# Sum passes from tables of three bfloat16 parts in a graph network kernel on Trainium2

## The chip, the cores and the metric

One core of a Trainium2 chip runs the whole kernel. The metric is device time in microseconds, the median of several runs. The engines are PE (TensorE, matrix products), VectorE (DVE), ScalarE (ACT), GpSimd (POOL), and SyncE (SP), which mostly issues DMAs.

## The reference

6250 nodes with 256 features and 100000 edges go through four graph layers, each followed by a residual and a layer norm. The change touches the last, two graph convolutions:

```
def gcn_conv(x, src, dst, W, b, n):
    h = x @ W
    ...
    norm = dinv[s] * dinv[d]
    msg = h[s] * norm[:, None]
    out = jax.ops.segment_sum(msg, d, num_segments=n)
    return out + b
...
x = gcn_conv(x, src, dst, W1, b1, n)          # 256 -> 128
x = jax.nn.relu(batch_norm(x, g1, be1))
...
x = gcn_conv(x, src, dst, W2, b2, n)          # 128 -> 64
x = jax.nn.relu(batch_norm(x, g2, be2))
...
return jax.nn.relu(cat @ Wfc + bfc)
```

`dinv` is the inverse root of a node's degree; self loops are in. So for each node the rows `h * dinv` of its neighbours are summed, times its own `dinv`.

## The kernel before

Nodes lie in 50 windows (NW) of 128, a window's node on a partition. Edges are sorted by target into 832 chunks of up to 128 edges; a chunk's targets all lie in one window. Eight chunks are a batch, 104 batches (NBT) a pass. Attention passes named a1e, a2e, be and te come first; the trace's tile names begin with the stage's name.

The stages around the change, in order:

- **g1l**, `dense_chain` with GROUP = 5 windows a group: finishes the attention layer, normalises, multiplies by W1, and drains each window twice (`drain_v`, L2749 and L2750): scaled by `dinv` into `tile`, which SP stores window by window into the table in DRAM, and into `acc`, where the sums begin. The steps of all engines are interleaved over `t`; a group's work on an engine is put at a fixed distance (T2, APPLY, SMALL) behind its first window.
- **g1e**, `sum_pass` with width 128. POOL gathers, chunk by chunk, the 128 table rows of its edges (L1830) into a ring of 6 batches. ScalarE makes one-hot matrices of target places (L1856, L1859), ring of 4. PE multiplies one-hot by rows (L1846) into one of 4 PSUM tiles of a batch. VectorE adds each chunk's product to its window in `acc` (L1874), at a place read from a table of window numbers (`windows.load`, L1124, every 4 batches), each add behind the one before.
- **g2l**, `turned_norm` with a table: transposes the sums, batch-normalises, then goes through 13 banks of four windows: ScalarE applies scale, shift and ReLU (L2357), PE multiplies by W2 (L2346), VectorE scales into `tile` (L2390) and `acc` (L2391), SP stores the tile (L2318). `tile` is a ring of two banks.
- **g2e**, `sum_pass` with width 64; then `turned_norm` n2 without a table, and the final dense stage gfl.

Each stage ends with a barrier of all engines, so POOL's first gather comes after the last store of the table has landed.

The lines that keep VectorE's ring of tiles in g2l:

```
for q in range(BANKS):
    dve.wait_ge(s_product, q + 1)
    wait(dve, s_stored[q % 2], q // 2 * 16)
    ...
    dve.tensor_tensor(tile[...], ps, factors(q, width), ALU.mult)
    dve.tensor_tensor(sums(q, width), ps, factors(q, width), ALU.mult).then_inc(s_v, 1)
```

## Time and profile before

| | us |
|---|---|
| median of 3 runs | 9034.76 |
| lowest, highest | 9013.13, 9043.17 |
| the profiled execution's own time | 9060.25 |
| its span | 9058.5 |
| g1l, from its first products to g1e's first gather | 6640 to 6777 |
| g1e, from its first gather | 6777 to 7823 |
| g2l | 7826 to 7870 |
| g2e, from its first gather | 7870 to 8915 |
| n2 and the final stage | to the end |

The profile shows one execution. A line of a group of instructions has the source line, the engine, the operation, out<-in, shapes and count, then busy time and mean length, then how long the engine stood idle before them and what it waited for. In the timeline each row has start, duration, and in brackets the idle time before it. A float32 product is two records. The granted PE clock is given as a share of 2.4 GHz.

### The profile page before, as it was taken

To read this page: it belongs to the slowest core of one execution; us is meant where nothing else is said; L and a number is where in the kernel's file an instruction comes from. 1 tells how busy PE (TensorE), PEld (TensorE's weight loads), DVE (VectorE), ACT (ScalarE), POOL (GpSimd) and SP (SyncE) were. 2 spreads that over 40 slices of the span, in tenths; PEclk is the share of its full clock that TensorE was granted. 3 is DMA by queue.
4 is the path that set the end of the run, shared out by engine and by line. 5 is a ranking of instruction groups with operands and counts; after the bars stand their busy time and mean duration, and the time that the engine had idled before them with its cause. 6 is when DMAs were issued, how large, how long until landed. Compare 5 with 4: busy or idle time off the path is not lost. (4 is left out here: it accounts for less than half of the span.)

```text
span 9058.5 us, 137581 instructions
## 1 busy us (share of the span) xinstructions
PE 5911.9 (65%) x32642; PEld 4085.2 (45%) x32642; DVE 5896.6 (65%) x17613; ACT 4188.0 (46%) x12362; POOL 6066.1 (67%) x6034
## 2 busy tenths in 40 slices
PE   5776567777688778567776777777764444433336
PEld 3443344454555555444444454555453333333335
DVE  8998688888588888556666699899972222211113
ACT  6897433333466666233333344444433333333332
POOL 7897377775588888177775166666647777577773
PEclk9998877777577777777777899999985555555557
DMA  1343255553333433144543366656622222111111
GB/s 47 112 116 104 73 135 137 136 135 93 79 93 93 112 94 93 60 129 133 133 132 106 117 174 174 173 170 176 174 83 53 53 53 53 42 27 27 27 27 40
DMA packets 518707, 903.05 MB, mean 100 GB/s; under 512 B 149412, under 2 KB 258878, under 8 KB 517565
## 3 DMA queue, kind: packets, MB, share of 16 engines
q0 software_dynamic: 226304, 550.69, 23.5%
q1 hardware_dynamic: 291644, 343.69, 12.6%
q8 instruction: 301, 4.93, 0.2%
q14 instruction: 458, 3.74, 0.1%
HBM read 820.41 MB, written 73.07 MB: 99 GB/s over the span
## 5 line engine op out<-in xcount | busy, mean ns | idle before, releaser
L1292 POOL DMA_INDIRECT all_Y<-table,all_row x3328 | 3413.4, 1026 | 1469.4 <-issue 966.4
L1830 POOL DMA_INDIRECT all_Y<-table,all_row x1664 | 1570.1, 944 | 548.8 <-issue 506.5
L1846 PE MATMUL g1e_ps_u<-all_Y,g1e_onehot 128*128 128x128 f32 x1664 | 428.8, 439 | 619.3 <-DMA all_Y<-table,all_row 422.8
L1846 PE MATMUL g2e_ps_u<-all_Y,g2e_onehot 128*128 128x64 f32 x1664 | 406.6, 426 | 639.2 <-DMA all_Y<-table,all_row 569.3
L1343 PE MATMUL be_ps_u<-all_Y,be_onehot 128*128 128x258 f32 x1664 | 655.3, 547 | 252.2 <-DVE all_acc L1556 245.6
L1874 DVE TENSOR_TENSOR all_acc<-all_acc,g1e_ps_u 128x128 f32 x832 | 238.8, 287 | 809.9 <-PE g1e_ps_u L1846 703.5
L1874 DVE TENSOR_TENSOR all_acc<-all_acc,g2e_ps_u 128x64 f32 x832 | 183.6, 221 | 864.3 <-PE g2e_ps_u L1846 757.8
L1343 PE MATMUL a1e_ps_u<-all_Y,a1e_onehot 128*128 128x264 f32 x1664 | 694.2, 546 | 4.8 <-DVE all_acc L1556 2.8
L1846 PEld LDWEIGHTS g1e_ps_u<-all_Y,g1e_onehot 128*128 128x128 f32 x1664 | 370.6, 328 | 677.3 <-issue 353.3
L1846 PEld LDWEIGHTS g2e_ps_u<-all_Y,g2e_onehot 128*128 128x128 f32 x1664 | 370.4, 328 | 675.4 <-issue 349.2
L1343 PEld LDWEIGHTS be_ps_u<-all_Y,be_onehot 128*128 128x128 f32 x1664 | 391.8, 264 | 480.7 <-issue 348.2
L1324 PE MATMUL te_ps_q<-all_X,te_turned 128*128 x1664 | 503.6, 431 | 154.4 <-DVE te_product L1594 132.5
L1343 PE MATMUL te_ps_u<-all_Y,te_onehot 128*128 128x264 f32 x1664 | 530.9, 434 | 80.7 <-DVE all_Y L1544 80.0
L638 POOL TENSOR_SCALAR all_acc<-all_Y,all_acc 128x128 f16<-128x128 f16 x392 | 488.7, 1258 | 47.4 <-DVE all_acc L625 33.9
L736 PE MATMUL a2e_rank_ps_p<-all_X 128*128 128x512 f16 (+1 forms) x1568 | 474.3, 456 | 0.0
L1324 PEld LDWEIGHTS te_ps_q<-all_X,te_turned 128*128 128x128 f32 x1664 | 322.8, 209 | 291.4 <-issue 251.2
L1544 DVE TENSOR_TENSOR all_Y<-all_Y 128x128 f32<-128x128 f32 (+1 forms) x728 | 377.7, 519 | 74.3 <-ACT all_Y L1468 54.6
L671 PE MATMUL rank_dst_ps_p<-all_acc 128*128 128x512 f16 (+1 forms) x1568 | 352.1, 347 | 104.5 <-POOL all_acc L638 104.1
L1343 PEld LDWEIGHTS a1e_ps_u<-all_Y,a1e_onehot 128*128 128x128 f32 x1664 | 375.6, 256 | 81.8 <-issue 11.8
L1343 PE MATMUL a2e_ps_u<-all_Y,a2e_onehot 128*128 128x66 f32 x1664 | 350.7, 348 | 90.8 <-DVE all_acc L1556 90.6
L1859 ACT ACTIVATE g1e_onehot<-g1e_distance 128x1024 f32<-128x1024 f16 x104 | 109.9, 1057 | 636.3 <-PE g1e_ps_u L1846 636.1
L1859 ACT ACTIVATE g2e_onehot<-g2e_distance 128x1024 f32<-128x1024 f16 x104 | 109.8, 1056 | 636.3 <-PE g2e_ps_u L1846 636.2
(555 smaller groups left out, 15694.2 us busy)
## 6 DMA issues: line engine op xcount, KB each, us to landing
all_Y<-table,all_row POOLq DMA_INDIRECT x4992, 2.5
a1e_place_row<-places_dst SPq DMA_DIRECT2D x104, 256.0 KB
a2e_place_row<-places_dst SPq DMA_DIRECT2D x104, 256.0 KB
be_place_row<-places_src SPq DMA_DIRECT2D x104, 256.0 KB
te_place_row<-places_src SPq DMA_DIRECT2D x104, 256.0 KB, 3.6
all_Y<-lows_dst SPq DMA_DIRECT2D x98, 256.0 KB
all_Y<-codes_dst SPq DMA_DIRECT2D x98, 256.0 KB
all_acc<-lows_src SPq DMA_DIRECT2D x98, 256.0 KB
```

The source lines that it names most:

```text
L638: pool.tensor_scalar(self.row1[b][:, k, :], self.kept.half16, self.row[b][:, k:k + 1], self.kept.other_t[:, t * 8 + k:t * 8 + k + 1], ALU. ...
L671: last = pe.matmul(ps[:, 0:a1 - a0], self.row1[b][:, k, :], self.column1[b][:, k, a0:a1], start=first, stop=final)
L736: last = pe.matmul(ps[:, 0:a1 - a0], self.row1[b][:, k, :], self.column1[b][:, k, a0:a1], start=first, stop=final)
L1292: pool.indirect_dma_start(out=rows[:, r, k, :], out_offset=None, in_=table, in_offset=bass.IndirectOffsetOnAxis(ap=order.row[:, t * 8 + k: ...
L1324: last = pe.matmul(ps_q[pair % 2][:, j * HC:(j + 1) * HC], turned[b][:, k * P:(k + 1) * P], queries[:, bass.ds(windows.at(windows_j, chunk ...
L1343: pe.matmul(ps_u[k % 4][:, 0:R], onehot[b][:, k, :], summand[:, b, k, :], start=True, stop=True).then_inc(s_summed, 1)
L1544: dve.tensor_tensor(out[:, :, :, 0:C], rows[:, r, ks, value_c0:value_c0 + HC].rearrange("p k (h n) -> p k h n", h=H), bc(by, [P, 2, H, C]) ...
L1830: pool.indirect_dma_start(out=rows[:, r, k, :], out_offset=None, in_=table, in_offset=bass.IndirectOffsetOnAxis(ap=order.row[:, t * 8 + k: ...
L1846: last = pe.matmul(ps_u[u][:, k * width:(k + 1) * width], onehot[b][:, k, :], rows[:, r, k, :], start=True, stop=True)
L1859: act.activation(onehot[t % MARKS][:, :, :], distance[:, :, :], ACT.Relu, scale=-1.0, bias=1.0).then_inc(s_onehot, 1)
L1874: dve.tensor_tensor(mine, mine, ps_u[(t - 1) % AHEAD][:, k * width:(k + 1) * width], ALU.add).then_inc(s_added, 1)
```

## The change

The tables of g1e and g2e hold each value as three bfloat16 parts, side by side: the first is the value rounded, the second the rest rounded, the third what is left. A gathered row has 3 x width bfloat16 (768 and 384 bytes; before 512 and 256). The one-hot matrices are bfloat16 too. PE makes one product per chunk with 384 or 192 columns, and VectorE adds its three parts one after the other to the window in `acc`. PSUM is cut into 8 banks, one chunk each for width 128 and two for width 64; PE releases chunks to VectorE by pairs and asks for free banks by pairs. The ring of rows has 4 batches for width 128, 6 for 64.

The dense stages make the parts. In g1l `acc` is the only drain; then, group by group, ScalarE copies `acc` into the first part, VectorE subtracts it into `rest`, ScalarE copies `rest` into the second, VectorE subtracts that into the third, and SP stores the group. In g2l the same is done bank by bank. Both write from a ring of two `split` buffers.

```diff
-    RING, AHEAD, MARKS, U = 6, 4, 4, 4
+    MARKS, U = 4, 4
+    RING = 4 if width == 128 else 6
+    BANKS = 8
+    PER = 512 // (3 * width)
+    ROUND = BANKS * PER
...
-        rows = spare[:, 0:RING * 8 * width].rearrange("p (r k n) -> p r k n", k=8, n=width)
-        onehot = [m.sb(f"onehot{b}", [P, 8, P]) for b in range(MARKS)]
+        rows = Region(spare).take(RING * 8, 3 * width, dt=BF16).rearrange("p (r k) n -> p r k n", k=8)
+        onehot = [m.sb(f"onehot{b}", [P, 8, P], BF16) for b in range(MARKS)]
...
+        def sums(q):
+            x = q % ROUND
+            return ps_u[x // PER][:, x % PER * 3 * width:(x % PER + 1) * 3 * width]
...
-                    wait(pe, s_added, (t - AHEAD + 1) * 8)
                     for k in range(8):
                         if k % 4 == 0:
                             pe.wait_ge(s_rows[r][k // 4], t // RING * 64 + 64)
-                        last = pe.matmul(ps_u[u][:, k * width:(k + 1) * width], onehot[b][:, k, :], rows[:, r, k, :], start=True, stop=True)
-                    last.then_inc(s_summed, 1)
+                        if k % 2 == 0:
+                            wait(pe, s_added, (t * 8 + k + 2 - ROUND) * 3)
+                        last = pe.matmul(sums(t * 8 + k), onehot[b][:, k, :], rows[:, r, k, :], start=True, stop=True)
+                        if k % 2 == 1:
+                            last.then_inc(s_summed, 1)
...
-                        wait(dve, s_added, t * 8 + (k - 8))
-                        dve.tensor_tensor(mine, mine, ps_u[(t - 1) % AHEAD][:, k * width:(k + 1) * width], ALU.add).then_inc(s_added, 1)
+                        if k % 2 == 0:
+                            dve.wait_ge(s_summed, (q + 2) // 2)
+                        for j in range(3):
+                            wait(dve, s_added, q * 3 + j)
+                            dve.tensor_tensor(mine, mine, sums(q)[:, j * width:(j + 1) * width], ALU.add).then_inc(s_added, 1)
```

In g1l (`dense_chain` with `split_of`), with `first_part` and `second_part` at steps T2 + 7 and T2 + 8 behind a group's start on ScalarE, `split_rest` and `split_last` at T2 + 8 and T2 + 9 on VectorE, the store at T2 + 10 on SP:

```diff
-                dve.tensor_scalar(tile[:, 0:128], ps[:, 0:128], dinv_of[:, w:w + 1], None, ALU.mult)
                 return dve.tensor_scalar(acc[:, w * 128:w * 128 + 128], ps[:, 0:128], dinv_of[:, w:w + 1], None, ALU.mult)
...
+                def first_part(g):
+                    act.wait_ge(s_v, (g + 1) * GROUP)
+                    wait(act, s_stored[g % 2], g // 2 * 16)
+                    act.activation(split[:, g % 2, :, 0:width2], split_of(g), ACT.Copy).then_inc(s_first, 1)
...
+                def second_part(g):
+                    act.wait_ge(s_rest, g + 1)
+                    act.activation(split[:, g % 2, :, width2:2 * width2], rest[:, :, :], ACT.Copy).then_inc(s_second, 1)
...
+                def split_rest(g):
+                    dve.wait_ge(s_first, g + 1)
+                    dve.tensor_tensor(rest[:, :, :], split_of(g), split[:, g % 2, :, 0:width2], ALU.subtract).then_inc(s_rest, 1)
...
+                def split_last(g):
+                    dve.wait_ge(s_second, g + 1)
+                    dve.tensor_tensor(split[:, g % 2, :, 2 * width2:3 * width2], rest[:, :, :], split[:, g % 2, :, width2:2 * width2], ALU.subtract).then_inc(s_split, 1)
```

In g2l (`turned_norm`), on SP, on ScalarE and on VectorE:

```diff
                     for q in range(BANKS):
-                        sp.wait_ge(s_v, q + 1)
+                        sp.wait_ge(s_split, q + 1)
...
+                    for q in range(BANKS + 1):
+                        if q < BANKS:
+                            act.wait_ge(s_v, q + 1)
+                            wait(act, s_stored[q % 2], q // 2 * 16)
+                            act.activation(split[:, q % 2, 0:windows(q), 0:width], sums(q, width), ACT.Copy).then_inc(s_first, 1)
+                        if q > 0:
+                            act.wait_ge(s_rest, q)
+                            act.activation(split[:, 1 - q % 2, 0:windows(q - 1), width:2 * width], rest[:, 0:windows(q - 1), :], ACT.Copy).then_inc(s_second, 1)
...
-                        wait(dve, s_stored[q % 2], q // 2 * 16)
...
-                        dve.tensor_tensor(tile[:, q % 2, 0:windows(q) * width].rearrange("p (w n) -> p w n", n=width), ps, factors(q, width), ALU.mult)
-                        dve.tensor_tensor(sums(q, width), ps, factors(q, width), ALU.mult).then_inc(s_v, 1)
+                    for q in range(BANKS + 2):
+                        if q < BANKS:
+                            dve.wait_ge(s_product, q + 1)
+                            ps = ps_o[q % 2][:, 0:windows(q) * width].rearrange("p (w n) -> p w n", n=width)
+                            dve.tensor_tensor(sums(q, width), ps, factors(q, width), ALU.mult).then_inc(s_v, 1)
+                        if q > 1:
+                            k = windows(q - 2)
+                            dve.wait_ge(s_second, q - 1)
+                            dve.tensor_tensor(split[:, q % 2, 0:k, 2 * width:3 * width], rest[:, 0:k, :], split[:, q % 2, 0:k, width:2 * width], ALU.subtract).then_inc(s_split, 1)
+                            dve.wait_ge(s_split, q - 1)
+                        if 0 < q <= BANKS:
+                            k = windows(q - 1)
+                            dve.wait_ge(s_first, q)
+                            dve.tensor_tensor(rest[:, 0:k, :], sums(q - 1, width), split[:, 1 - q % 2, 0:k, 0:width], ALU.subtract).then_inc(s_rest, 1)
```

How this moves instructions is shown at three places. The first is VectorE at the start of g1e, before (TENSOR_LOAD reads the window numbers, ISA is the register instruction that computes a window's place, ps_u0 is a PSUM tile):

```order
L1124 TENSOR_LOAD all_window
L1874 ISA
L1874 TENSOR_TENSOR all_acc<-all_acc,g1e_ps_u0 128x128
L1874 ISA
L1874 TENSOR_TENSOR all_acc<-all_acc,g1e_ps_u0 128x128
```

And the same place with the change:

```order
L1124 TENSOR_LOAD all_window
L1887 ISA
L1887 TENSOR_TENSOR all_acc<-all_acc,g1e_ps_u0 128x128 x3
L1887 ISA
L1887 TENSOR_TENSOR all_acc<-all_acc,g1e_ps_u1 128x128 x3
```

Where one add followed each register instruction, three do, and the next chunk is in the next bank.

The second is VectorE in g2l's banks, before (two banks):

```order
L2390 TENSOR_TENSOR g2l_tile<-g2l_ps_o0,all_small 128x256
L2391 TENSOR_TENSOR all_acc<-g2l_ps_o0,all_small 128x256
L2390 TENSOR_TENSOR g2l_tile<-g2l_ps_o1,all_small 128x256
L2391 TENSOR_TENSOR all_acc<-g2l_ps_o1,all_small 128x256
```

And with the change, the first four banks' drains (L2450), the subtractions into `rest` (L2459) and the third parts (L2454):

```order
L2450 TENSOR_TENSOR all_acc<-g2l_ps_o0,all_small 128x256
L2450 TENSOR_TENSOR all_acc<-g2l_ps_o1,all_small 128x256
L2459 TENSOR_TENSOR g2l_rest<-all_acc,g2l_split 128x256
L2450 TENSOR_TENSOR all_acc<-g2l_ps_o0,all_small 128x256
L2454 TENSOR_TENSOR g2l_split<-g2l_rest,g2l_split 128x4x64
L2459 TENSOR_TENSOR g2l_rest<-all_acc,g2l_split 128x256
L2450 TENSOR_TENSOR all_acc<-g2l_ps_o1,all_small 128x256
L2454 TENSOR_TENSOR g2l_split<-g2l_rest,g2l_split 128x4x64
L2459 TENSOR_TENSOR g2l_rest<-all_acc,g2l_split 128x256
```

The tile's drain is gone, and a bank's third part stands behind the drain of the bank two later.

The third is ScalarE in g2l. Before, its work there ends with the thirteen L2357 (in the changed kernel L2408). With the change first parts (L2414) and second parts (L2417) follow:

```order
L2408 ACTIVATE all_Y<-all_Y,g2l_column 128x512 x12
L2408 ACTIVATE all_Y<-all_Y,g2l_column 128x256
L2414 ACTIVATE g2l_split<-all_acc 128x4x64 x2
L2417 ACTIVATE g2l_split<-g2l_rest 128x4x64
L2414 ACTIVATE g2l_split<-all_acc 128x4x64
L2417 ACTIVATE g2l_split<-g2l_rest 128x4x64
L2414 ACTIVATE g2l_split<-all_acc 128x4x64
L2417 ACTIVATE g2l_split<-g2l_rest 128x4x64
```

The first parts of banks 0 and 1 come together; from then on the first part of a bank stands ahead of the second part of the bank before.

## Rows read from the trace of the kernel before

**Rows 1.** The page: each engine's busy time, share of the span and instructions.

```profile
PE 5911.9 (65%) x32642; PEld 4085.2 (45%) x32642; DVE 5896.6 (65%) x17613; ACT 4188.0 (46%) x12362; POOL 6066.1 (67%) x6034
```

**Rows 2.** Windows: part of a1e, of a2e, g1l, part of g1e, of g2e.

```profile
core 0: us, PE busy (x) PEld busy (x) DVE busy (x) ACT busy (x) POOL busy (x), PEclk, DMA share, GB/s
1200.00:1800.00 600.00, 469.96 (x2229) 299.04 (x2229) 526.21 (x1584) 236.38 (x767) 453.95 (x475) 0.77 0.51 136
2400.00:3000.00 600.00, 491.07 (x4051) 336.67 (x4050) 484.93 (x1987) 410.02 (x1328) 482.51 (x386) 0.71 0.39 98
6640.00:6777.00 137.00, 95.27 (x584) 81.65 (x584) 109.36 (x335) 52.20 (x214) 48.06 (x60) 0.90 0.18 66
6790.00:7790.00 1000.00, 412.88 (x1603) 356.72 (x1602) 230.19 (x802) 350.89 (x901) 755.89 (x802) 0.50 0.21 53
...
7890.00:8890.00 1000.00, 390.99 (x1600) 356.20 (x1600) 176.58 (x800) 344.05 (x883) 755.76 (x801) 0.50 0.15 27
```

**Rows 3.** Timeline rows of g1e and g2e, and groups by line and form.

```profile
7302.91 2.05 PE L1846 MATMUL g1e_ps_u<-all_Y,g1e_onehot 128*128 128x128 f32 x8 [3.09 <-DMA all_Y<-table,all_row]
7307.74 0.94 POOL L1830 DMA_INDIRECT all_Y<-table,all_row  x1 [0.30 <-issue]
7309.95 3.30 DVE L1874 TENSOR_TENSOR all_acc<-all_acc,g1e_ps_u 128x128 f32 x8 [6.34 <-PE g1e_ps_u L1846]
7883.62 2.76 DVE L1874 TENSOR_TENSOR all_acc<-all_acc,g2e_ps_u 128x64 f32 x8 [16.56 <-PE g2e_ps_u L1846]
L1859 ACT ACTIVATE g1e_onehot<-g1e_distance 128x1024 f32<-128x1024 f16 x104 | 109.9, 1057 | 636.3 <-PE g1e_ps_u L1846 636.1
L736 PE MATMUL a2e_rank_ps_p<-all_X 128*128 128x512 f16 x784 | 401.4, 519 | 0.0
```

**Rows 4.** Adds and loads by line (ns min/median/max), and a dependent VectorE chain in g2l.

```profile
L1874 DVEq FUSED_REGOPS  x1664: 57/57/57, 6790.7 to 8914.7; - x185
L1874 DVE TENSOR_TENSOR all_acc<-all_acc,g1e_ps_u x832: 286/286/289, 6790.8 to 7822.3; 128x128 f32 x167
L1124 DVEq TENSOR_LOAD <-all_window x188: 1096/2101/2350, 1152.3 to 8904.9; - x188
7841.35 0.19 DVE L2375 TENSOR_TENSOR g2l_parts<-g2l_parts 128x26 f32<-128x26 f32 x1
7841.57 0.19 DVE L2376 TENSOR_TENSOR g2l_parts<-g2l_parts,g2l_stats 128x26 f32<-128x26 f32 x1
```

**Rows 5.** Timeline of g2l: ScalarE's L2357, banks 10 and 12, the first gather.

```profile
7843.75 9.06 ACT L2357 ACTIVATE all_Y<-all_Y,g2l_column 128x512 f32<-128x512 f32 x13 [7.62 <-DVE g2l_column L2384]
7863.75 0.42 DVE L2390 TENSOR_TENSOR g2l_tile<-g2l_ps_o,all_small 128x256 f32<-128x256 f32 x1 [0.95 <-PE g2l_ps_o L2346]
7864.09 0.41 DVE L2391 TENSOR_TENSOR all_acc<-g2l_ps_o,all_small 128x256 f32<-128x256 f32 x1
7865.46 0.43 DVE L2390 TENSOR_TENSOR g2l_tile<-g2l_ps_o,all_small 128x256 f32<-128x256 f32 x1 [0.95 <-PE g2l_ps_o L2346]
7866.57 0.29 DVE L2390 TENSOR_TENSOR g2l_tile<-g2l_ps_o,all_small 128x128 f32<-128x128 f32 x1 [0.36 <-DMA table<-g2l_tile]
7866.78 0.28 DVE L2391 TENSOR_TENSOR all_acc<-g2l_ps_o,all_small 128x128 f32<-128x128 f32 x1
7870.26 0.99 POOL L1830 DMA_INDIRECT all_Y<-table,all_row  x1 [27.20 <-SPq L1823]
```

**Rows 6.** g1l's drains and tail on the timeline, and prices from groups by form.

```profile
6760.99 0.34 DVE L2750 TENSOR_SCALAR all_acc<-g1l_ps_o,all_small 128x128 f32<-128x128 f32 x1
6761.25 0.34 DVE L2749 TENSOR_SCALAR g1l_tile<-g1l_ps_o,all_small 128x128 f32<-128x128 f32 x1
6773.25 0.35 DVE L2749 TENSOR_SCALAR g1l_tile<-g1l_ps_o,all_small 128x128 f32<-128x128 f32 x1 [2.12 <-DMA table<-g1l_tile]
L2742 DVE TENSOR_TENSOR all_Y<-all_acc 128x1280 f32<-128x1280 f32 x10 | 14.9, 1492 | 0.3
L2357 ACT ACTIVATE all_Y<-all_Y,g2l_column 128x256 f32<-128x256 f32 x1 | 0.6, 586 | 0.0
```

More of the change, by code:

```diff
@@ L2006, in dense_chain @@
             cuts2 = [(a, min(a + 512, width2)) for a in range(0, width2, 512)]
-            tile = m.sb("tile", [P, 2, B.table_width])
+            if split_of is None:
+                tile = m.sb("tile", [P, 2, B.table_width])
+            else:
+                tile = None
+                split = m.sb("split", [P, 2, GROUP, 3 * width2], BF16)
+                rest = m.sb("rest", [P, GROUP, width2])
+                s_first, s_rest, s_second, s_split = (m.sem(x) for x in ("first", "rest", "second", "split"))
         if norm:
@@ L2044, in _ @@
                     w = t - T2 - 2
-                    if B is not None and is_window(w):
+                    g = group_at(t - T2 - 10)
+                    if split_of is not None and g is not None:
+                        sp.wait_ge(s_split, g + 1)
+                        sp.dma_start(B.table[g * GROUP * P:(g + 1) * GROUP * P, :].rearrange("(w p) n -> p w n", p=P), split[:, g % 2, :, :]).then_inc(s_stored[g % 2], 16)
+                    if split_of is None and B is not None and is_window(w):
                         sp.wait_ge(s_v, w + 1)
@@ L2249, in _ @@
                 for t in range(STEPS):
+                    if split_of is not None and group_at(t - T2 - 9) is not None:
+                        split_last(group_at(t - T2 - 9))
                     if B is not None and is_window(t - T2 - 2):
                         drain2(t - T2 - 2)
+                    if split_of is not None and group_at(t - T2 - 8) is not None:
+                        split_rest(group_at(t - T2 - 8))
                     if A is not None and is_window(t - T1 - 2):
@@ L2290, in turned_norm @@
             W = m.sb("W", [P, width])
-            tile = m.sb("tile", [P, 2, 4 * width])
+            split = m.sb("split", [P, 2, 4, 3 * width], BF16)
+            rest = m.sb("rest", [P, 4, width])
+            s_first, s_rest, s_second, s_split = (m.sem(x) for x in ("first", "rest", "second", "split"))
             ps_o = [m.ps(f"ps_o{b}", [P, 512]) for b in range(2)]
@@ L2755, in gnn_kernel @@
                         second=Step(sources=[(x3, 0, P), (x3, P, P)], weights=[W[:, 0, :], W[:, 1, :]], width=128, drain_v=drain_v,
-                                    table=tables[128], table_width=128))
-        sum_pass(nc, c, "g1e", order, tables[128], 128, acc, T2)
-        turned_norm(nc, c, "g2l", 128, acc, dinv_of, T1, (g_b1, g_g1, g_be1), g_w2, tables[64], 64)
-        sum_pass(nc, c, "g2e", order, tables[64], 64, acc, T2)
+                                    table=split_tables[128], table_width=384),
+                        split_of=lambda g: acc[:, g * GROUP * 128:(g + 1) * GROUP * 128].rearrange("p (w n) -> p w n", n=128))
+        sum_pass(nc, c, "g1e", order, split_tables[128], 128, acc, T2)
+        turned_norm(nc, c, "g2l", 128, acc, dinv_of, T1, (g_b1, g_g1, g_be1), g_w2, split_tables[64], 64)
+        sum_pass(nc, c, "g2e", order, split_tables[64], 64, acc, T2)
         turned_norm(nc, c, "n2", 64, acc, dinv_of, T2, (g_b2, g_g2, g_be2), ones_row=True)
```

34 lines of the change are left out of this document (19 added, 15 removed).

## The prediction

> **What bounds the kernel now.** I read the page's busy shares, then stretches of time (windows), then the groups and single instructions of the stages that change. No engine is busy more than 67% of the span [rows 1], so the shares name no bound; each stage must be read by itself. Both sum passes, g1e and g2e, show the same picture [rows 2]: POOL 756 of 1000 us busy, VectorE 230 and 177, PE 413 and 391, ScalarE 351 and 344. POOL is busy for 0.94 us, then 0.30 us in "issue", then starts the next gather [rows 3]; 1000 us hold 802 gathers, so they start 1.25 us apart, and nothing is waited for. 832 gathers make 1040 us a pass, and that is the pass. PE waits for landings, VectorE for PE [rows 3]. It makes no difference that g1e gathers 512 bytes a row and g2e 256: the pace is one.
>
> The stages between are another matter. In g1l VectorE is busy 109 of 137 us [rows 2]. In g2l's second half PE makes one bank of four windows in 1.71 us, VectorE drains it with two instructions [rows 5], and stores stay behind that.
>
> **The change part by part.**
>
> *Products.* Four chunks' float32 products, two records each, take 2.05 us [rows 3]. A product becomes one bfloat16 product with 384 or 192 columns. The nearest row, 128x512 in float16, has 0.519 us [rows 3]; even at that, eight products take 4.2 us of a batch's 9.98. PE waited anyhow: worth 0. PE's clock is already granted at 0.50 in both passes, its lower level of 1.2 GHz [rows 2], so less work there has little to lose.
>
> *Adds.* VectorE now adds three parts per chunk. Eight adds take 3.30 us in g1e, so one takes (3.30 - 0.29) / 7 = 0.43 us from start to start: 0.286 of work, 0.057 of a register instruction that computes the window's place, and two hand-overs of 0.04 [rows 3, 4]. The second and third add reuse that place, and only wait for the add before. A chain of such dependent instructions in g2l leaves 0.03 us between them [rows 4], so I take 0.286 + 0.035 = 0.32 us. A chunk costs 0.43 + 2 x 0.32 = 1.07 us, a batch 8.6, plus a quarter of the 2.1 us load of window numbers [rows 4]: 9.1 us against POOL's 9.98. In g2e eight adds take 2.76 us [rows 3], 0.54 less, so 24 take 1.6 less: 7.5. Covered, with 0.9 us a batch to spare; the rings of rows (now four batches) and banks only need to bridge a half batch. The tail of a pass moves by under 1 us: there are three times the adds, but the first pair starts before all four products are done. Worth 0 for both passes, 1 us either way.
>
> *Gathers.* Same number and same indices. Rows grow to 768 and 384 bytes. a1e's rows are 1056 bytes, and its gathers come every 600 / 475 = 1.26 us [rows 2]. Worth 0.
>
> *g1l.* VectorE loses one drain per window. The start-to-start distance of L2750 and the next L2749 is 0.26 us [rows 6], so 1.3 us a group. It gains two subtractions of 640 elements a group: half of 1280 elements at 1.492 is 0.75 [rows 6], and with a small instruction's 0.19 [rows 4] on top of the half's own fixed part it is at most 0.85. Net +0.2 to +0.4 us for nine groups: +2.5 us. ScalarE gets two copies of 640 elements a group, halfway between 256 at 0.586 and 1024 at 1.057 [rows 3, 6], 0.82; it is busy 52 of 137 us, and that idle time hides them. Without that cover they cost up to 15 us. The tenth group is at the tail, where nothing hides it. Today the last drain there waits 2.12 us for a store [rows 6], which goes, about 2.4 us gained in all. Then come copy, subtract, copy, subtract: 0.82 + 0.75 + 0.82 + 0.75 and four hand-overs, 3.3 us. Then the store: 480 KB where there was 64 KB. a1e moves 136 GB/s at half DMA share [rows 2]; 416 KB more are 3.1 us at that rate and 1.6 at twice that; I take 2.5. Tail +3.4, g1l in all **+6 us**, from -1 to +15.
>
> *g2l.* Here is the cost. The table is written from a ring of two buffers, as before. But ScalarE's queue is now: first part of bank q, then second part of bank q-1 (the order above). The first part of bank q waits for the store of bank q-2. The store of bank q-2 is only issued after VectorE's last subtraction of that bank. What is queued behind that wait on ScalarE is the second part of bank q-1, which VectorE's last subtraction of q-1 needs, and so the store of q-1. So this is a loop with one store's whole latency per bank: store, first copy, second copy, last subtraction. The store's latency stands in the trace: bank 10's L2391 ends at 7864.50, and bank 12, which waits for its buffer, starts at 7866.57 [rows 5]: 2.07 us, hand-overs included, for 128 KB. I add 0.15 for 192 KB. A copy of 256 elements lies between a quarter of 1024 at 1.057, 0.264 [rows 3], and 0.586, the row with scale and bias [rows 6]; I take 0.47, nearer the row of the same size. The subtraction has 0.41, as L2391 [rows 5], and 0.07 go for hand-overs. Period: 2.22 + 0.94 + 0.48 = **3.64 us** against 1.71.
>
> ScalarE can't begin before its thirteen L2357 are done, 7843.75 + 9.06 = 7852.81 [rows 5]. Bank 0's first copy, subtraction, second copy and last subtraction (0.47, 0.41, 0.47, 0.41 and hand-overs) hand it over at 7854.75. Eleven periods later, at 7894.8, bank 11; the last, half a bank, 1.1 us later, 7895.9. Today that point is 7866.78 + 0.28 = 7867.06, and the first gather starts 3.2 us after it [rows 5]. So g2l costs **+29 us**. Lower end: copies 0.264 each, no more for the larger store, VectorE at its 0.34 start to start, a period of 3.0 and +22. Upper end: copies 0.586, the store 2.6, a period of 4.3 and +36.
>
> That a store costs about two microseconds whatever its size is also in the Trainium skill ("DMA: Bandwidth & Descriptors", Anatomy of one DMA): a fixed 2.0 us, mostly the wait for the written bytes' receipt, and bytes by 436 GB/s. By that, 192 KB would be an estimated 2.45 us, the period 3.87 and g2l +31; the trace's 2.07 us for 128 KB lies a little under its 2.3.
>
> **The sum.** Profiled execution: 9060.25 + 6 (g1l) + 29 (g2l) + 0 (passes) = 9095 us. It is 25.5 above the median of the runs, 9034.76, so I predict **9070 us** there, +35, with the ends of g1l and g2l 9056 to 9086. About 0.3%, 27 us, is what a measurement here can tell from no change; the border is 9062, so the forecast is slower, but close to it.
>
> **The rivals.**
>
> *A: the store loop does not bind g2l, and the time is the same.* If the buffer were free when ScalarE asks, PE would go on at 1.71 us a bank; g2l would only lose the late start of ScalarE and the last bank's four steps, some 5 us. With g1l that gives 9035 + 11 = **9046 us**. For it: today the same ring of two makes VectorE wait only once [rows 5]. Against it: today a bank's store is issued right after its drain, a bank and a half before the buffer is wanted; now it is issued by the step behind the one that waits. It decides at a period of 3.0 us: under that g2l costs less than 21 us, and the whole less than 27.
>
> *B: VectorE becomes the bound of g1e.* If the second and third add cost what the first does (0.43), a batch takes 24 x 0.43 + 0.53 = 10.85 us against 9.98: 0.87 x 104 = 90 us more, **9160 us**. g2e stays covered (1.6 less, 9.25). It begins above (9.98 - 0.53 - 8 x 0.43) / 16 = 0.376 us an add, a gap of 0.09 where I take 0.035. For it: no row shows two dependent adds from PSUM without the register instruction. Against it: the short chain, and 0.43 itself is 0.286 + 0.057 + two gaps of 0.04.
>
> *C: a busy VectorE slows the gathers.* VectorE goes from 23% to some 85%. In a2e POOL needs 600 / 386 = 1.55 us a gather, with VectorE 81% busy; in a1e 1.26 with VectorE 88% busy [rows 2]. So it is not the share but the kind of instruction. At a2e's pace both passes would take 1664 x 0.304 = 506 us more, **9576 us**. The adds here have a1e's kind: float32, one operand in PSUM. The Trainium skill ("SBUF — State Buffer", SBUF: two separate sides) has a rule for this: VectorE and GpSimd hold a shared pair of ports in turn, and VectorE takes it in its two-port modes or with two SBUF inputs. By that rule these adds, with one SBUF input, leave POOL alone; a1e agrees.
>
> *D: faster.* g1l would have to gain more than g2l loses: all drains' 13 us without the subtractions would not do it. Only the spread of the runs can make it look so.
>
> **How the numbers follow.** Forecast 0.76, A 0.12, B 0.08, C 0.02, D 0.02. Inside the forecast, by its ends and the runs' spread of 30 us, about a quarter falls below 9062. Slower: 0.76 x 0.76 + 0.10 = 0.68; same: 0.18 + 0.12 = 0.30; faster 0.02. The range 9040 to 9105 holds the forecast with some spread of runs, and A; B and C, and the outer tails, are left out.
>
> **What would show it.** Right: gathers in both passes 1.25 us apart, with POOL 756 of 1000 us; VectorE 80 to 90% busy in g1e, its second and third adds 0.32 us apart; in g2l one store each 3.6 us, ScalarE waiting for the DMA before each first part, and PE idle; g1l's first gather some 6 us later after its start, g2l's some 29 later. Wrong: g2l's banks at 1.7 us (A); g1e's gathers in groups with waits for PE (B); gathers over 1 us long while the adds run (C).

## The result and the profile after

| | us |
|---|---|
| before, median of 7 runs | 9039.02 (9013.13 to 9053.15) |
| after, median of 7 runs | 9073.52 (9044.98 to 9076.28) |
| ratio, with its 95% interval | 1.0033 (1.0021 to 1.0045) |
| after, the profiled execution | 9044.98, span 9043.3 |

The change costs 34.5 us, 0.33%. The profiled execution of the changed kernel happens to be the fastest of its seven, and that of the kernel before, 9060.25, lies above all seven shown here. Compared as totals, the two profiles would say "15 us faster". That difference lies ahead of the change: g1l begins 46.9 us earlier in the profile of the changed kernel, and 32 of these are in a2e, which the change doesn't touch (1283.4 us from its first product of gathered rows to its last in the one, 1251.0 in the other). So the stages must be compared one by one, each from its own landmark:

| stage, from what to what | before | after | difference | predicted |
|---|---|---|---|---|
| g1l, first add to `all_X` to first gather | 124.16 | 129.63 | +5.5 | +6 |
| g1e, first gather to g2l's first SyncE transfer | 1048.27 | 1048.19 | -0.1 | 0 |
| g2l, that transfer to the next first gather | 44.85 | 71.01 | +26.2 | +29 |
| g2e, first gather to n2's first SyncE transfer | 1048.28 | 1048.24 | 0.0 | 0 |
| sum | | | +31.6 | +35 |

The 3 us between this sum and the medians' 34.5 can't be assigned: the interval of the ratio stands for 19 to 41 us.

The page's engine row of the changed kernel, the counterpart of [rows 1]:

```profile
PE 5532.6 (61%) x30978; PEld 3533.3 (39%) x30978; DVE 6740.9 (75%) x20924; ACT 4210.4 (47%) x12408; POOL 6037.3 (67%) x6034
```

PE lost 379 us of work and VectorE gained 844. Neither lengthens the passes: POOL, which didn't change, still paces both. Windows of g1e and g2e of the changed kernel (start and end, us, then PE, PEld, VectorE, ScalarE, POOL busy, PE clock, DMA share, GB/s), and g1e's groups by line:

```profile
6740.00:7740.00 1000.00, 289.94 (x800) 86.70 (x800) 686.72 (x2392) 359.18 (x923) 756.31 (x801) 0.50 0.30 79
7860.00:8860.00 1000.00, 162.00 (x801) 86.76 (x802) 529.81 (x2400) 358.45 (x921) 755.88 (x802) 0.50 0.19 40
```

```profile
L1838 POOL DMA_INDIRECT all_Y<-split,all_row x829 | 783.7, 945 | 252.5 <-issue 252.5
L1887 DVE TENSOR_TENSOR all_acc<-all_acc,g1e_ps_u 128x128 f32 x2487 | 714.2, 287 | 334.6 <-PE g1e_ps_u L1855 159.4 <-DVE all_acc L1887 54.7 <-issue 4.1
L1855 PE MATMUL g1e_ps_u<-all_Y,g1e_onehot 128*128 128x384 bf16 x832 | 301.5, 517 | 749.6 <-DMA all_Y<-split,all_row 381.8 <-issue 367.8
```

Against [rows 2]: PE 413 to 290, VectorE 230 to 687, POOL 756 both times, with 801 or 802 gathers in 1000 us. POOL's only idle time is "issue", so no gather waited for a free buffer. VectorE still waits for PE 159 us, where it waited 703 before. Not all of that is slack: VectorE's own load of window numbers (2.1 us every fourth batch) and the hand-over after PE lie inside these waits.

The passes' near-zeros in the table hide a shift at the pass's end. The end of g1e, first in the kernel before, then in the changed one:

```profile
7814.50 0.94 POOL L1830 DMA_INDIRECT all_Y<-table,all_row  x1 [0.30 <-issue]
7820.57 2.00 DVE L1874 TENSOR_TENSOR all_acc<-all_acc,g1e_ps_u 128x128 f32 x5 [0.20 <-DVE all_acc L1874]
7825.41 0.33 SPq L2313 DMA_DIRECT2D g2l_vector<-in_L_gnn_b  x1
```

```profile
7781.16 2.00 DVE L1887 TENSOR_TENSOR all_acc<-all_acc,g1e_ps_u 128x128 f32 x6 [0.21 <-DVE all_acc L1887]
7783.93 0.34 SPq L2364 DMA_DIRECT2D g2l_vector<-in_L_gnn_b  x1
```

Counted from the first gather, the last add ends 2.0 us later than before (1047.4 us instead of 1045.4), but g2l's first transfer follows 0.8 us behind it instead of 2.8. In the kernel before that transfer comes 10.91 us after the last gather's start, and so it does, within 0.01 us, in g2e of both kernels and of every undisturbed variant below. What sets this time stays open. In g1e of the changed kernel it is 9.4 us, and the adds end the pass.

g2l is where the time went. Two periods of its banks in the changed kernel, VectorE, ScalarE and the store queue:

```profile
7812.57 0.43 DVE L2454 TENSOR_TENSOR g2l_split<-g2l_rest,g2l_split 128x256 bf16<-128x256 f32 x1
7813.02 3.82 SPq L2369 DMA_DIRECT2D split<-g2l_split  x2
7813.03 0.42 DVE L2459 TENSOR_TENSOR g2l_rest<-all_acc,g2l_split 128x256 f32<-128x256 f32 x1
7813.37 0.42 DVE L2450 TENSOR_TENSOR all_acc<-g2l_ps_o,all_small 128x256 f32<-128x256 f32 x1
7815.26 0.42 ACT L2414 ACTIVATE g2l_split<-all_acc 128x256 bf16<-128x256 f32 x1 [2.72 <-DMA split<-g2l_split]
7815.58 0.40 ACT L2417 ACTIVATE g2l_split<-g2l_rest 128x256 bf16<-128x256 f32 x1
7816.01 0.42 DVE L2454 TENSOR_TENSOR g2l_split<-g2l_rest,g2l_split 128x256 bf16<-128x256 f32 x1 [2.22 <-ACT g2l_split L2417]
```

Here is the loop (L2414 makes a first part, L2417 a second, L2454 a third): third part of bank 0 at 7812.57, its store right behind it, ScalarE waiting 2.72 us for that store, first part of bank 2, second part of bank 1, third part of bank 1 at 7816.01, 3.44 us after that of bank 0. From bank 0 (7812.57) to bank 11 (7850.17) the third parts come 3.42 us apart on average. The waits of the tile `g2l_split` (us, times):

```profile
  DMA split<-g2l_split: 29.8, 11
  ACT g2l_split L2417: 25.0, 12
```

Eleven waits of 2.7 us each for a store, and twelve of VectorE for ScalarE behind them. In [rows 5] there was one wait for a store, of 0.36 us.

g1l's tail in the changed kernel, with the chain of four steps that nothing hides:

```profile
6727.84 0.74 ACT L2205 ACTIVATE g1l_split<-all_acc 128x640 bf16<-128x640 f32 x1 [1.71 <-DVE all_acc L2818]
6728.60 0.82 DVE L2286 TENSOR_TENSOR g1l_rest<-all_acc,g1l_split 128x640 f32<-128x640 f32 x1 [0.80 <-ACT g1l_split L2205]
6729.46 0.74 ACT L2209 ACTIVATE g1l_split<-g1l_rest 128x640 bf16<-128x640 f32 x1 [0.89 <-DVE g1l_rest L2286]
6730.23 0.83 DVE L2290 TENSOR_TENSOR g1l_split<-g1l_rest,g1l_split 128x640 bf16<-128x640 f32 x1 [0.80 <-ACT g1l_split L2209]
6731.08 0.36 SPq L2067 DMA_DIRECT2D split<-g1l_split  x1
6735.74 1.05 POOL L1838 DMA_INDIRECT all_Y<-split,all_row  x1 [19.73 <-SPq L1831]
```

Copy, subtraction, copy, subtraction: 3.2 us, then a store of 480 KB that takes 2.9 us to land (64 KB took 1.5 before), then the first gather.

### The profile page after: what moved, and what is told of

It reads as the page before. It is cut to its first block and busy times, and to the rows that moved or that the text cites. A ratio compares the mean times of both kernels' runs of the same rounds, so it can differ in the third digit from the quotient of the medians.

```text
span 9043.3 us, 138372 instructions
## 1 busy us (share of the span) xinstructions
PE 5532.6 (61%) x30978; PEld 3533.3 (39%) x30978; DVE 6740.9 (75%) x20924; ACT 4210.4 (47%) x12408; POOL 6037.3 (67%) x6034
## 5 line engine op out<-in xcount | busy, mean ns | idle before, releaser
L1292 POOL DMA_INDIRECT all_Y<-table,all_row x3328 | 3380.8, 1016 | 1461.5 <-issue 962.6
L1838 POOL DMA_INDIRECT all_Y<-split,all_row x1664 | 1571.6, 944 | 579.5 <-issue 506.4
L1887 DVE TENSOR_TENSOR all_acc<-all_acc,g1e_ps_u 128x128 f32 x2496 | 716.8, 287 | 335.3 <-PE g1e_ps_u L1855 159.4
L1887 DVE TENSOR_TENSOR all_acc<-all_acc,g2e_ps_u 128x64 f32 x2496 | 551.0, 221 | 496.3 <-PE g2e_ps_u L1855 333.1
L1855 PE MATMUL g1e_ps_u<-all_Y,g1e_onehot 128*128 128x384 bf16 x832 | 301.5, 517 | 749.6 <-DMA all_Y<-split,all_row 381.8
L1855 PE MATMUL g2e_ps_u<-all_Y,g2e_onehot 128*128 128x192 bf16 x832 | 168.4, 357 | 888.2 <-DMA all_Y<-split,all_row 459.1
L1855 PEld LDWEIGHTS g1e_ps_u<-all_Y,g1e_onehot 128*128 128x128 bf16 x832 | 90.2, 128 | 960.5 <-issue 477.3
L1556 DVE TENSOR_TENSOR all_acc<-all_acc,te_ps_u 128x264 f32 x832 | 346.1, 416 | 82.2 <-issue 54.5
L1869 ACT ACTIVATE g1e_onehot<-g1e_distance 128x1024 bf16<-128x1024 f16 x104 | 109.9, 1056 | 637.4 <-PE g1e_ps_u L1855 637.2
L1869 ACT ACTIVATE g2e_onehot<-g2e_distance 128x1024 bf16<-128x1024 f16 x104 | 109.9, 1057 | 635.0 <-PE g2e_ps_u L1855 634.9
```

The lines of the kernel that those rows point to most:

```text
L1292: pool.indirect_dma_start(out=rows[:, r, k, :], out_offset=None, in_=table, in_offset=bass.IndirectOffsetOnAxis(ap=order.row[:, t * 8 + k: ...
L1556: dve.tensor_tensor(mine, mine, ps_u[k % 4][:, 0:R], ALU.add).then_inc(s_added, 1)
L1838: pool.indirect_dma_start(out=rows[:, r, k, :], out_offset=None, in_=table, in_offset=bass.IndirectOffsetOnAxis(ap=order.row[:, t * 8 + k: ...
L1855: last = pe.matmul(sums(t * 8 + k), onehot[b][:, k, :], rows[:, r, k, :], start=True, stop=True)
L1869: act.activation(onehot[t % MARKS][:, :, :], distance[:, :, :], ACT.Relu, scale=-1.0, bias=1.0).then_inc(s_onehot, 1)
L1887: dve.tensor_tensor(mine, mine, sums(q)[:, j * width:(j + 1) * width], ALU.add).then_inc(s_added, 1)
```

## The experiments

The theory: g2l's cost is a loop through ScalarE's queue, with a store's whole latency in it; the passes are paced by POOL, and VectorE's three adds hide under it. The rivals: PE or VectorE paces g2l's banks; the adds are part of the passes' time. The first four kernels below were run once each, beside one run of the kernel before (9014.4 us). Their totals vary by as much as most of the effects, so each is read by its stages; a stage that a variant doesn't touch repeats within 0.7 us.

**Four split buffers in g2l (9038.09 us).**

```diff
-            split = m.sb("split", [P, 2, 4, 3 * width], BF16)
+            SPLITS = 4
+            split = m.sb("split", [P, SPLITS, 4, 3 * width], BF16)
...
-                            wait(act, s_stored[q % 2], q // 2 * 16)
+                            wait(act, s_stored[q % SPLITS], q // SPLITS * 16)
```

> The changed kernel with four split buffers in g2l instead of two; nothing else differs. Theory (g2l pays one store's latency per bank because the first part of a bank waits for the store of the bank two before): the wait for stores goes, the banks follow each other at 1.7 us (PE) or slightly less while they catch up, and g2l from its first SyncE DMA to g2e's first gather falls from 71.0 us to about 52 us, 19 us less. Rival (the chain of copies and subtractions itself makes the 3.4 us per bank): g2l stays at 71 us. g1l (129.6 us from its first add to the first gather) and both passes (1048.2 us from first gather to the next stage's first DMA) unchanged.

From g1e's first gather to g2e's took 1099.03 us, where the changed kernel had 1119.20: 20.2 less. By its own landmarks g2l is 50.4 us, 20.6 less than the changed kernel's 71.0. Its banks in the timeline:

```profile
7833.93 0.42 DVE L2455 TENSOR_TENSOR g2l_split<-g2l_rest,g2l_split 128x256 bf16<-128x256 f32 x1
7834.05 0.42 ACT L2415 ACTIVATE g2l_split<-all_acc 128x256 bf16<-128x256 f32 x1 [0.50 <-DVE all_acc L2451]
7834.84 0.42 ACT L2418 ACTIVATE g2l_split<-g2l_rest 128x256 bf16<-128x256 f32 x1 [0.38 <-DVE g2l_rest L2460]
7835.30 0.42 DVE L2451 TENSOR_TENSOR all_acc<-g2l_ps_o,all_small 128x256 f32<-128x256 f32 x1 [0.49 <-PE g2l_ps_o L2398]
7835.64 0.41 DVE L2455 TENSOR_TENSOR g2l_split<-g2l_rest,g2l_split 128x256 bf16<-128x256 f32 x1
```

No wait for a store is left. The third parts are 1.71 us apart, PE's pace of [rows 5], and VectorE waits for PE again. The store loop was 20 of the 26 us. The rival, that the chain of copies and subtractions makes the 3.4 us a bank, falls.

**Second part ahead of the first part, still two buffers (9045.51 us).**

```diff
                     for q in range(BANKS + 1):
+                        if q > 0:
+                            act.wait_ge(s_rest, q)
+                            act.activation(split[:, 1 - q % 2, 0:windows(q - 1), width:2 * width], rest[:, 0:windows(q - 1), :], ACT.Copy).then_inc(s_second, 1)
                         if q < BANKS:
...
-                        if q > 0:
-                            act.wait_ge(s_rest, q)
-                            act.activation(split[:, 1 - q % 2, 0:windows(q - 1), width:2 * width], rest[:, 0:windows(q - 1), :], ACT.Copy).then_inc(s_second, 1)
```

> The changed kernel with ScalarE's two copies in g2l in the other order: the second part of bank q-1 ahead of the first part of bank q; two buffers as before. Theory: the loop then holds two banks, 2.3 (store) + 0.4 + 0.4 + 0.4 + 0.4 and hand-overs = 4.1 us for two, 2.1 us a bank instead of 3.42, so g2l falls by about 11 x 1.3 = 14 us to 57 us. Rival (ring of two alone sets it, whatever stands in the queue): stays at 3.4 a bank and 71 us.

Gather to gather 1105.19 us, 14.0 less than the changed kernel; g2l is 56.5 by its own landmarks, 14.5 less. This is the test of the queue itself: no buffer was added and no work taken away, two instructions only changed places. What stands behind the wait now belongs to the same bank as the wait:

```profile
7829.68 0.42 ACT L2417 ACTIVATE g2l_split<-all_acc 128x256 bf16<-128x256 f32 x1 [1.36 <-DMA split<-g2l_split]
7830.65 0.42 ACT L2413 ACTIVATE g2l_split<-g2l_rest 128x256 bf16<-128x256 f32 x1 [0.56 <-DVE g2l_rest L2459]
7831.03 0.42 ACT L2417 ACTIVATE g2l_split<-all_acc 128x256 bf16<-128x256 f32 x1
...
7833.77 0.42 ACT L2417 ACTIVATE g2l_split<-all_acc 128x256 bf16<-128x256 f32 x1 [1.33 <-DMA split<-g2l_split]
```

The store's latency is met every second bank instead of every bank, so two banks take 4.09 us, and ScalarE waits for stores 6 times and 8.0 us in all, instead of 11 times and 29.8, by order alone.

**One add per chunk (9048.04 us).** The second and third part are left out of the sums, and PE's wait for a free bank counts one add per chunk instead of three.

```diff
-                        for j in range(3):
-                            wait(dve, s_added, q * 3 + j)
+                        for j in range(1):
+                            wait(dve, s_added, q * 1 + j)
```

> The changed kernel in which VectorE adds only the first of the three parts of each chunk; the second and third parts are left out of both sums. Theory (the passes stand on POOL's gathers, the adds are covered): VectorE's busy time in g1e falls to a third, and both passes stay at 1048.2 us within 1 us. Rival (the added VectorE work costs something in the passes, by waits of PE or by slower gathers): the passes get shorter by several us.

**Four adds per chunk (9256.02 us).** The first part is added once more, so the sums come out wrong; PE's wait counts four.

```diff
-                        for j in range(3):
-                            wait(dve, s_added, q * 3 + j)
-                            dve.tensor_tensor(mine, mine, sums(q)[:, j * width:(j + 1) * width], ALU.add).then_inc(s_added, 1)
+                        for j in range(4):
+                            wait(dve, s_added, q * 4 + j)
+                            dve.tensor_tensor(mine, mine, sums(q)[:, j % 3 * width:(j % 3 + 1) * width], ALU.add).then_inc(s_added, 1)
```

> The changed kernel with a fourth add per chunk, the first part once more, so that sums are changed. It measures how near VectorE is to being the bound. Two chunks take 2.22 us in g1e now, 1.81 in g2e; a further dependent add costs 0.32 and 0.26. So a chunk becomes 1.43 us in g1e and 1.17 in g2e against POOL's 1.248. Theory: g1e grows to 832 x 1.43 + 26 loads of 2.1 us = about 1245 us (+200), g2e with 1.17 + 0.07 for the loads stands right at 1.24, +0 to +15 us. Rival (further adds are hidden or overlap): both passes unchanged; rival (adds cost 0.43 each): g1e +290 us.

With one add, g1e took 1045.43 us instead of 1048.19. The gathers kept their pace; the 2.8 us are the pass's end, where the last adds have no gathers to hide under. The expectation of at most 1 us missed this. g2e didn't get shorter (1048.63 us instead of 1048.24): its last add ends earlier, and n2's first transfer still comes 10.91 us after the last gather. With four adds, the last add comes 1247.8 us after the first gather, where it came 1047.2 after it: +200.6. g2e stayed at 1048.22. Windows of g1e, first the kernel with one add, then the one with four, under them a stretch of the latter's timeline, and last two rows of the changed kernel for comparison:

```profile
6750.00:7750.00 1000.00, 289.38 (x799) 86.53 (x800) 229.16 (x799) 355.34 (x913) 756.40 (x800) 0.50 0.29 79
```

```profile
6760.00:7960.00 1200.00, 326.15 (x808) 55.03 (x808) 922.55 (x3221) 349.77 (x900) 775.98 (x821) 0.50 0.25 68
```

```profile
7203.49 2.64 DVE L1887 TENSOR_TENSOR all_acc<-all_acc,g1e_ps_u 128x128 f32 x8 [0.21 <-DVE all_acc L1887]
...
7206.35 2.65 DVE L1887 TENSOR_TENSOR all_acc<-all_acc,g1e_ps_u 128x128 f32 x8 [0.21 <-DVE all_acc L1887]
...
7207.29 0.95 POOL L1838 DMA_INDIRECT all_Y<-split,all_row  x1 [1.75 <-PE g1e_ps_u L1855]
```

```profile
7203.13 2.00 DVE L1887 TENSOR_TENSOR all_acc<-all_acc,g1e_ps_u 128x128 f32 x6 [0.73 <-PE g1e_ps_u L1855]
7205.35 2.00 DVE L1887 TENSOR_TENSOR all_acc<-all_acc,g1e_ps_u 128x128 f32 x6 [0.21 <-DVE all_acc L1887]
```

The second and third add together cost 2.8 us at the pass's end. The fourth costs 200 us, by the mechanism of rival B: over g1e VectorE waits for PE only 14.5 us (159 in the changed kernel), and POOL waits 184.5 us for PE to free a row buffer. The price per add comes out of it too. Eight adds (two chunks) start 2.86 us apart here and six 2.22 in the changed kernel, so an add that only follows another is (2.86 - 2.22) / 2 = 0.32 us. A batch of 24 adds is 4 x 2.22 = 8.9 us, with the window numbers' load (2.1 every fourth batch) 9.4 us, of POOL's 9.98. The cover is 0.6 us a batch, 6%. The same working with 2.86 gives 12.0 us a batch and 1244 us a pass, and the kernel with four adds took 1248.8. VectorE's "69% busy" hides this, since the gaps between dependent adds are not counted as busy: a queue can be 94% full at 69% busy.

**Two repairs: g2l's ReLUs interleaved, g1l's subtractions on GpSimd.** The first variant takes the ring of four and also lets ScalarE start its split copies after four of its thirteen ReLUs (L2408). The second moves g1l's two subtractions a group from VectorE to GpSimd; with them ScalarE's second copy and the store come two steps later. The third does both.

```diff
-                for q in range(BANKS):
+                def relu(q):
                     act.activation(T[0:n, part(q)], T[0:n, part(q)], ACT.Relu, scale=scale, bias=shift).then_inc(s_applied, 1)
+
+                EARLY = 4 if table is not None else BANKS
+                for q in range(EARLY):
+                    relu(q)
                 if table is not None:
                     for q in range(BANKS + 1):
+                        if q + EARLY < BANKS:
+                            relu(q + EARLY)
...
```

> Four split buffers in g2l, and ScalarE applies only four of its thirteen ReLUs ahead, the rest between the split copies. Theory (g2l's cost is the store loop, and after it the late start of ScalarE's first parts behind all thirteen ReLUs): g2l falls from 71.0 us, over the 50.8 of the ring of four alone, to 46 to 48, at most 3 above the kernel before's 44.9; from g1e's first gather to g2e's first gather some 1095, the whole some 24 us under the changed kernel and 10 (0 to 15) above the kernel before. Rival (the ring of four had already taken all that can be had, since PE or VectorE sets the pace of a bank, not ScalarE's start): g2l stays at 50.8, the whole 20 us under the changed kernel.

```diff
+                    if split_of is not None and g >= 5:
+                        split_rest(pool, g - 5)
...
+                    if split_of is not None and g >= 5:
+                        split_last(pool, g - 5)
...
-                    if split_of is not None and group_at(t - T2 - 9) is not None:
-                        split_last(group_at(t - T2 - 9))
...
-                    if split_of is not None and group_at(t - T2 - 8) is not None:
-                        split_rest(group_at(t - T2 - 8))
...
-                    if split_of is not None and group_at(t - T2 - 8) is not None:
-                        second_part(group_at(t - T2 - 8))
+                    if split_of is not None and group_at(t - T2 - 10) is not None:
+                        second_part(group_at(t - T2 - 10))
```

> g1l's two subtractions a group on GpSimd instead of VectorE. Theory (g1l is bound by VectorE, and the change took five drains a group off it and put two subtractions on): VectorE loses 1.6 us a group, so the nine groups come some 15 us earlier, the tail grows by 2 to 3 us, since a subtraction of 640 elements is about 1.9 us on GpSimd; g1l from its first add to g1e's first gather falls from 129.6 to 115 to 119. Rival (GpSimd's subtractions hold up VectorE's two-input instructions, or they come late on GpSimd's own queue, and the gain is given back): g1l 125 us or more, with VectorE's instructions longer while GpSimd subtracts.

> The interleaved ReLUs with four buffers in g2l and the subtractions on GpSimd in g1l, together. Theory: both gains add, -24 in g2l and -10 to -14 in g1l against the changed kernel: some 36 us under it, 5 us (0 to 15) under the kernel before, ratio to that one 0.998 to 1.001. Rival: only the part in g2l is kept, and it stands some 10 us above the kernel before, ratio 1.001.

These three met a disturbed chip: the kernel before itself took 10634.43 us beside them (nine runs, 10629.85 to 10669.67), and the traces of the variants have gaps ahead of the instructions of the gathering passes. The dense stages were not touched: g1l of the interleaved kernel, which has the changed kernel's g1l, took 129.5 us (the changed kernel 129.6). So the dense stages can be read, and the totals can't. The totals were 10947.93 (ratio 1.0288, 1.0269 to 1.0307), 10956.52 for the kernel with GpSimd alone, and 10913.9 (1.0261, 1.0243 to 1.028) for both.

g2l with the interleaved ReLUs took 47.9 us (9409.65 to 9457.54), and the same with both. The theory's 46 to 48 holds, and the rival's 50.8 falls: ScalarE's late start was worth another 2.5 us. g1l with GpSimd subtracting took 124.1 us, and 122.8 with both: under the rival's 125, over the theory's 115 to 119. Both missed.

**GpSimd alone once more (10820.22 us; the kernel before 10507.18 beside it).**

> The subtractions of g1l on GpSimd once more, since the kernel before itself took 10634 us where it had 9014 in the first call, with gaps before the instructions of every engine. Expected with the kernel before near 9040 us: by the theory g1l from its first add to g1e's first gather 115 to 119 us instead of 129.6, by the rival 125 or more.

The disturbance was still there. g1l took 122.8 us, g2l 71.0, as in the changed kernel.

**The kernel before and both repairs, undisturbed.**

> The kernel before, unchanged, for a trace of it from the same call. In the last two calls it took 10634 and 10507 us where it had 9014 in the first. If the chip is as in those: by the theory (only the supply of instructions is slower then, so a pass with 24 adds a batch on VectorE is no longer hidden and one with 8 adds still is) the kernel before has both passes at 1048 us, with gathers 1.25 us apart, and the changed kernel has them at some 1350. By the rival (the gathers themselves are slower) both kernels' passes are longer alike. If the chip is as in the first call: both passes 1048 us and the whole near 9040.

> The interleaved ReLUs with four buffers in g2l and the subtractions on GpSimd in g1l, once more. With the kernel before near 9040 us: g2l 47.9 us instead of the changed kernel's 71.0 and the kernel before's 44.9, g1l from its first add to the first gather 122.9 instead of 129.6 and 124.2, both as its first trace has them, so 30 us under the changed kernel and 2 above the kernel before, ratio 0.999 to 1.002. With the kernel before near 10500: 2.6 to 3 per cent above it, as in its first call, all of it in the two passes.

The kernel before took 9021.61 us in its profiled execution and 9030.35 at the median of thirteen runs. Its stages repeat: g1l 123.6 us, g1e 1048.2, g2l 44.8, g2e 1048.3. Both repairs together took 9031.76 us, ratio 1.0001 (0.9992 to 1.0011), where the changed kernel has 1.0033 (1.0021 to 1.0045). Its stages are g1l 123.0, g1e 1048.0, g2l 47.9 and g2e 1048.3. All that the change cost is won back, and no more: both expectations hold. This version doesn't beat the kernel before; nothing in it touches POOL's 1040 us a pass.

Why the subtractions, 1.65 us a group less on VectorE, brought only 0.9 us a group (93.9 to 95.1 us from the first drain to the last, instead of 102.2) shows in this last kernel's g1l. First two of its groups by line in the stretch of the drains, then the timeline of one group of windows, and L2280 in a group where GpSimd is idle:

```profile
L2280 DVE TENSOR_SCALAR all_X<-all_X,g1l_columns 128x256 f32<-128x256 f32 x27 | 17.3, 694 | 0.0
L2827 DVE TENSOR_SCALAR all_acc<-g1l_ps_o,all_small 128x128 f32<-128x128 f32 x49 | 16.7, 342 | 9.8 <-PE g1l_ps_o L2169 9.8
```

```profile
6675.13 2.37 DVE L2280 TENSOR_SCALAR all_X<-all_X,g1l_columns 128x256 f32<-128x256 f32 x3
6675.15 3.65 POOL L2824 TENSOR_TENSOR all_X<-all_X,g_bias 128x256 f32<-128x256 f32 x5
...
6678.68 1.49 DVE L2820 TENSOR_TENSOR all_Y<-all_acc 128x1280 f32<-128x1280 f32 x1
...
6678.75 2.68 POOL L2046 TENSOR_TENSOR g1l_split<-g1l_rest,g1l_split 128x640 bf16<-128x640 f32 x1
...
6707.52 1.05 DVE L2280 TENSOR_SCALAR all_X<-all_X,g1l_columns 128x256 f32<-128x256 f32 x3
```

And in the changed kernel:

```profile
L2818 DVE TENSOR_SCALAR all_acc<-g1l_ps_o,all_small 128x128 f32<-128x128 f32 x49 | 16.7, 341 | 5.4 <-PE g1l_ps_o L2155 5.3
L2266 DVE TENSOR_SCALAR all_X<-all_X,g1l_columns 128x256 f32<-128x256 f32 x27 | 15.3, 620 | 0.0
```

Nine groups of two subtractions were 14.8 us of VectorE. Of these 2.0 were lost because in five groups the third L2280 now runs beside GpSimd's L2824 and takes 0.81 us instead of 0.40, 4.4 to waits for PE, so the drains end 8.1 us earlier. The tail is 1.6 longer (the last drain to the first gather 9.9 us instead of 8.3): the two subtractions in it take 1.4 us each on GpSimd and 0.8 on VectorE. VectorE set the pace of g1l, but PE stood close behind it.

## Why the prediction was right

The forecast was 9070 us, +35, slower; it is 9073.52, +34.5. The range 9040 to 9105 holds it. The mechanism was the forecast one, a store's latency in each turn of a loop through ScalarE's queue. That the totals agree within 0.5 us is luck: the stages' sum is 31.6 against 35, and the interval is 19 to 41 us. Point by point:

- **The store loop in g2l** was the step that mattered, and both halves of it are shown: with four buffers the banks go at PE's 1.71 us, and with the order turned round 6 of the 11 waits for stores are left, with 8.0 of their 29.8 us. Its size was a little over: a period of 3.64 us was forecast and 3.42 is measured (7812.57 to 7850.17 in eleven banks). The term that was mis-sized is the two copies. I put them one behind the other at 0.47 each, 0.94. In the trace they are 0.42 and 0.40, the second starts 0.32 after the first, and both together, up to the next subtraction, are 0.75. The store was 2.26 us, end of the third part to start of the next first part, where I took 2.22. The Trainium skill's fit ("DMA: Bandwidth & Descriptors", Anatomy of one DMA) gives an estimated 2.45 us for 192 KB. The section fits DMAs that GpSimd issues, which the prediction didn't say, and these stores are SyncE's; the trace stays under the fit here, and near it for g1l's 480 KB store, an estimated 3.1 against 2.9.
- **The rest of g2l**, the late start of ScalarE and the last bank's steps, was part of the sum but not named as a price of its own except under rival A ("some 5 us"). With the loop gone g2l is 50.4, 5.5 above 44.9; of those, 2.5 go with the ReLUs interleaved.
- **g1l** was forecast at +6 and came at +5.5. Copies 0.74 instead of 0.82, subtractions 0.82 to 0.83 instead of 0.75, a chain of 3.2 us instead of 3.3, a larger store worth 1.4 (1.5 to 2.9 to land), not 2.5. The first nine groups cost some 3.2 instead of 2.5, the tail some 2.3 instead of 3.4. The errors are small and partly cancel.
- **The adds** were forecast at 0.32 us for the second and third, and they are 0.32. The chunk is 1.11 us instead of 1.07, since its first add has 0.46 from start to start, not 0.43: it now also waits for PE's pair. A batch is 9.4 us instead of 9.1, and the cover 0.6 instead of 0.9. "VectorE 80 to 90% busy" was wrong as a sign to look for: I counted the gaps as busy. It is 69% busy, and its queue is 94% full.
- **The passes' ends** were put at under 1 us. The changed kernel's last add ends 2.0 us later in g1e, and one add a chunk instead of three makes the pass 2.8 shorter. That g1e still came out at -0.1 is luck in this step: the kernel before waits 2.1 us longer between its last add and g2l's first transfer, for a reason that stays open.
- **The gathers**: POOL 756 of 1000 us and 0.945 us each in both passes, against [rows 2], with rows of 768 and 384 bytes. Rival C falls. The Trainium skill's rule that VectorE takes the shared pair of ports only in its two-port modes or with two SBUF inputs ("SBUF — State Buffer", SBUF: two separate sides) holds for these adds.
- **Rival A** would have needed a period under 3.0 us; it is 3.42. **Rival B** falls for three adds, and the kernel with four shows its mechanism at full size.
- **The products**: PE has 123 us less to do in g1e and nothing comes of it, since it waited before and waits now.

## What to carry to other kernels

When a wait for a buffer is put into an in-order queue, look at what stands behind it: if that is the work that leads to the very store being waited for next, each turn pays the store's whole latency. Here a longer ring took all of that away (20.6 us), and the order of two lines more than half (14.5). Taking work off PE or putting it on VectorE is worth nothing in a stage that another engine's queue paces, but it uses up cover; reckon the cover from start-to-start distances, not from busy shares. Compare stages between landmarks, because two profiled executions of the same code differ by as much as such a change.

## What the runs showed of the hardware

**The same three instructions take 1.05 or 2.37 us, depending on GpSimd.** The three L2280 in the rows above are 2.37 us while GpSimd adds the bias (L2824, both inputs and output in SBUF) and 1.05 in the group where it is idle. The other way round, GpSimd's subtraction of 640 elements is 1.39 us by itself and 2.68 when VectorE's L2820, with two SBUF inputs, runs beside it. So moving work to GpSimd isn't free for VectorE. The Trainium skill's rule on the shared ports ("SBUF — State Buffer", SBUF: two separate sides) counts an operation like L2280, a tensor_scalar from SBUF to SBUF, among those that can take a two-port mode, and L2820 has two SBUF inputs; these rows agree with it.

**On a disturbed chip the passes with three adds a chunk lost more.** Beside the disturbed runs of the kernel before, the changed kernel's variants stood 2.6 to 3.0% above it instead of 0 to 0.3%. g1e of the interleaved kernel took 1354.9 us instead of 1048, and g2e 1349.7. Its window of g1e, and single adds in it:

```profile
8070.00:9070.00 1000.00, 246.74 (x612) 41.36 (x612) 521.20 (x1818) 270.39 (x696) 596.63 (x631) 0.50 0.22 62
```

```profile
8507.11 0.29 DVE L1887 TENSOR_TENSOR all_acc<-all_acc,g1e_ps_u 128x128 f32 x1 [0.42 <-DVE all_acc L1887]
8507.95 0.29 DVE L1887 TENSOR_TENSOR all_acc<-all_acc,g1e_ps_u 128x128 f32 x1 [0.55 <-DVE all_acc L1887]
8509.25 0.29 DVE L1887 TENSOR_TENSOR all_acc<-all_acc,g1e_ps_u 128x128 f32 x1 [1.01 <-DVE all_acc L1887]
8510.66 0.29 DVE L1887 TENSOR_TENSOR all_acc<-all_acc,g1e_ps_u 128x128 f32 x1 [1.13 <-issue]
```

An add is still 0.29 us and a gather 0.95, and half of the gaps between adds are still the usual 0.03 us, but between them stand gaps of 0.4 to 1.1 us, as in these rows; one gap in ten is 1 us or more. POOL then waits for PE (272 us over g1e), and PE for VectorE (861), as with four adds. What slows the hand-overs stays open. No trace shows the kernel before disturbed, so what follows is inferred from totals. The interleaved kernel was 313.5 us over the kernel before; 8 of them are g1l and g2l, and the other stages run the same code, so its two passes took some 305 us more than the kernel before's. These then took some 1200 us each instead of 1048: they weren't spared either, and lost about half of what the passes with three adds did. Nor were g1e and g2e alone: from its first tile to its last, a2e took 1815 us in the interleaved kernel and 1278 in the changed one. That fits neither the theory that only the passes with 24 adds a batch suffer nor the rival that both kernels' passes are longer alike.
